# Fused adaLN block: the feed-forward input turned by VectorE block transposes through DRAM instead of by TensorE

## Chip, cores and metric

The kernel runs on one core of a Trainium2 chip. The metric is the device time of one launch in microseconds. TensorE (PE) does the matrix products, VectorE (DVE) and ScalarE (ACT) the elementwise work, GpSimd (POOL) adds and subtracts, and SyncE (SP) issues nearly all DMAs.

## What is computed

Input x is (1, 8192, 512). Two halves follow each other, each behind a LayerNorm with a scale and a shift that come from a modulation vector:

```python
mod = (silu(c) @ wmod)                # sa, ca, ga, sb, cb, gb, each 512 long
h = layernorm(x) * (1 + ca) + sa
x = x + ga * linear_attention(h)      # 16 heads of 32, causal, float32
h = layernorm(x) * (1 + cb) + sb
hid = silu(h @ wg.T) * (h @ wu.T)     # wg, wu: (1536, 512), integer words / 127
x = x + gb * (hid @ wd.T)             # wd: (512, 1536)
```

Products are made with float32 operands split into a high and a low part.

## The kernel before

**Layout.** The attention half goes over 16 groups of 512 tokens and leaves its output in DRAM as `x_mid`. The feed-forward half goes over FG = 8 groups G of 1024 tokens (FT = 8 tiles of 128 tokens) and over HB = 12 blocks q of 128 hidden features. A product needs the features on the partitions, whereas `x_mid` is loaded with the tokens on the partitions. So the normalized x has to be turned: per group eight banks (four feature chunks c, two halves of 512 tokens), each of four 128x128 transposes.

**One step q** (`step` in `tensor`, L1939) is seven products p1, p7, p2, p5, p4, p6, p3 of four matmuls each (a scheme with seven products in place of eight), written by `product` (L1862, its matmul is L1868). p7 and p4 are those of block q-1. ScalarE copies partial results out of PSUM (`save_p1`, `save_p5`, `save_u2`, L1565 to L1578), applies silu (L1583, L1590), and makes the high part of the hidden values (`h_high`, L1595). VectorE adds (`add_c11` L1704, `add_c12` L1710, `add_c22` L1715) and gates (`times_gate1` L1721, `times_gate2` L1729). GpSimd makes the low parts (`h_low`, L1497). What VectorE does for the next group stands in `aside(q)`, between `times_gate1(q-1)` and `add_c12(q)`.

**The down-projections.** After steps 5 and 11 TensorE runs eight of them (`down`, L1910, matmul L1925), numbered i = 0 to 7 and 8 to 15, each of 12 matmuls into one of four banks `dn`. The last p7 and p4 lie between the first ones. `down(G, i)` waits until VectorE has scaled bank i-4 (`gate_y`, L1736). GpSimd then adds the residual (L1502) and SP stores the tile.

**The turn before.** `load_x` (L1396) brings the tiles of group G+2 into `xg` once TensorE has turned group G+1. VectorE takes the statistics in steps 2 to 5 (`norm_stats`, L1681), GpSimd the power -1/2 (`rstd_of`, L1492), VectorE normalizes in place (`norm_x`, L1697) behind `add_c12(6)` and in steps 7 to 9. TensorE turns (`turn`, L1930, transposes L1936) banks 0, 1 and 2 at the ends of steps 8, 9 and 10, bank 3 at the end of step 11, and banks 4 to 7 between down-projections 9 and 11. ScalarE carries each bank with scale and shift to SBUF (`evacuate`, L1562).

**Behind step 11** ("the tail" below) the next group's operands are made: sums T1 to T4 on VectorE (`sum_of`, L1671), high parts on ScalarE (`high`, L1547), low parts on VectorE (`low`, L1675), each for k = 0 and 1. VectorE's order there is written out by hand (L1808 to L1837): twelve sums and low parts and three of the last step's instructions stand ahead of `gate_y(8)`, more between `gate_y(8)`, `(9)` and `(10)`. Only then do down-projections 12, 13 and 14 find their banks free.

**Where the halves meet.** The x of feed-forward group 0 is loaded during attention groups g = 14 and 15 by one 1 MB DMA each (L404), whose statistics are taken in `norm_stats` of the attention part (L757); it is turned by TensorE (L1097, L1105).

Of the kernel before, what the change touches and what calls it, by code (L numbers as in the profile page):

```python
# [43 lines left out]
Shared = namedtuple("Shared", "xg xf h_hi h_lo ring b_hi b_lo full wd silu_sum saved gate h y x_res gb_row pairs sums dn")  # L44
# [24 lines left out]
def build(nc, x, w_qkv, b_qkv, b_cols, w_out, b_out, c_vec, c_row, w_mod, w_mod_t, ffn_words, out):  # L69
    top = ExitStack()  # L70
    with top:
# [10 lines left out]
        k_dram = nc.dram_tensor("k_dram", (P, D), F32, kind="Internal").ap()  # L82
        gb_dram = nc.dram_tensor("gb_dram", (1, D), F32, kind="Internal").ap()
# [60 lines left out]
        ffn = feed_forward(sem, later, ident, mod_col, half_neg, norm, gb_dram, parts, att, shared, x_mid, out)  # L144
# [40 lines left out]
def attention(nc, s, sem, sbuf, psum, ident, gb_dram, mod_col, half_neg, w_hi, w_lo, xt_hi, xt_lo, ga_row,  # L185
# [5 lines left out]
    z_exp = sbuf(s, "z_exp", [P, 2, GN])  # L191
    z_relu = sbuf(s, "z_relu", [P, 2, GN])
# [40 lines left out]
    v_ready, ksum_ready, prod_ready, prod_turned = sem("v_ready"), sem("ksum_ready"), sem("prod_ready"), sem("prod_turned")  # L233
# [26 lines left out]
    shared = Shared([xg[:, t, :] for t in range(GT)] + [z[:, i, :] for z in (z_exp, z_relu) for i in range(2)],  # L260
# [42 lines left out]
    def sync(sp, first_loads):  # L303
# [90 lines left out]
        def group(g, parity):  # L394
# [4 lines left out]
            else:  # L399
# [4 lines left out]
                sp.dma_start(xg[:, :, :], mid_groups[half, :, :, :]).then_inc(x_in, 16)  # L404
# [348 lines left out]
    def vector(dve, sum_of, low):  # L753
        def norm_stats(g, tiles=range(GT)):
            wait(dve, x_in, 16 * (g + 1))
# [568 lines left out]
def feed_forward(sem, later, ident, mod_col, half_neg, norm, gb_dram, parts, att, shared, x_mid, out):  # L1324

    stats, mean_var, var_eps, rstd = norm[1:5]
    xg, xf, h_hi, h_lo, (blocks, filled), b_hi, b_lo, full, wd, total, saved, gate, h, y, x_res, gb_row, xs, sums, dn = shared
# [8 lines left out]
    xt_ps, xf_ready = sem("fxt_ps"), sem("fxf_ready")  # L1336
    gb_in, gb_chain, gb_done = sem("gb_in"), sem("gb_chain"), sem("gb_done")
# [50 lines left out]
    def sync(sp):  # L1388
# [95 lines left out]
    def gpsimd(pool):  # L1484
# [24 lines left out]
        def body(G):  # L1509
            ahead = not isinstance(G, int) or G + 1 < FG  # L1510
            for q in range(HB):
                if q not in (5, 11):
                    h_low(G, q, 1)
                    h_low(G, q, 0)
                if q == 5:
                    h_low(G, q, 1)
                    h_low(G, q, 0)
                    if ahead:
                        rstd_of(G + 1)
# [18 lines left out]
    def scalar(act):  # L1538
# [10 lines left out]
        def evacuate(G, i, bank):  # L1549
# [511 lines left out]
```

## Time and profile before

| | us |
|---|---|
| median of 3 runs | 1996.96 |
| lowest, highest | 1995.05, 2000.71 |
| the profiled execution, its whole time | 1998.45 |
| its span, first to last instruction | 1996.7 |

The mean granted clock of TensorE in the profiled execution is 0.998 of full speed. Attention ends and the feed-forward half begins near 1000 us. A timeline row gives the start, the duration, the engine, the line, the instruction with its output and inputs, how many were merged, and in brackets the idle time before it with what ended it. The programs' names are those of the tensors' memory: pj and sc are PSUM banks of the products, num, sc and state those of the down-projections.

### The profile page before, as it was taken

What the parts mean: (1) busy time and instruction counts of PE and PEld (TensorE: products, weight loads), DVE (VectorE), ACT (ScalarE), POOL (GpSimd) and SP (SyncE); (2) the same over time, 40 slices, a digit from 0 to 9 for tenths busy, and PEclk for the clock granted to TensorE, in tenths of its full rate; (3) what the DMA queues carried; (4) which work ended last, traced back from release to release, by engine and by line L of the source; (5) the groups of instructions that cost most, each with busy time, mean ns of one, the idle gap of its engine ahead of it and who ended that gap; (6) DMA issues with size and microseconds to landing.
All of it is one profiled execution on the core that took longest, in us unless ns stands there. A gap on an engine that the chain in (4) does not pass through costs nothing. (4 is left out here: it accounts for less than half of the span.)

```text
span 1996.7 us, 43856 instructions
## 1 busy us (share of the span) xinstructions
PE 1960.6 (98%) x16008; PEld 1591.9 (80%) x16008; DVE 1443.1 (72%) x2386; ACT 905.7 (45%) x1542; POOL 877.4 (44%) x718
## 2 busy tenths in 40 slices
PE   7999999999999999999899999999999999999999
PEld 4788888888888888887678888788888888888887
DVE  7977888878788878787865857658576585765744
ACT  5443444344444434443344535445354453544533
POOL 2533544444544444453334443444434444344444
PEclk9999999999999999999999999999999999999999
DMA  7223333444434434432575654656546565465553
GB/s 268 69 91 102 115 123 119 135 130 133 135 100 133 128 125 135 127 110 90 179 263 176 207 187 145 214 170 209 186 144 215 171 210 186 144 214 174 169 168 106
DMA packets 202521, 309.81 MB, mean 155 GB/s; under 512 B 16145, under 2 KB 72977, under 8 KB 202386
## 3 DMA queue, kind: packets, MB, share of 16 engines
q1 hardware_dynamic: 201858, 306.78, 48.1%
q8 instruction: 107, 1.75, 0.4%
q10 hardware_dynamic: 528, 1.05, 0.1%
q14 instruction: 28, 0.23, 0.0%
HBM read 225.19 MB, written 82.58 MB: 154 GB/s over the span
## 5 line engine op out<-in xcount | busy, mean ns | idle before, releaser
L1497 POOL TENSOR_TENSOR h_lo<-y_rows,h_hi 128x512 fp32r<-128x512 f32 x192 | 246.5, 1301 | 367.6 <-ACT h_hi L1595 367.6
L461 POOL TENSOR_TENSOR x_res<-y,x_res 128x512 f32<-128x512 f32 x64 | 86.6, 1353 | 294.0 <-DVE y L872 283.5
L851 DVE TENSOR_TENSOR probs<-sc,causal 128x512 f32<-128x512 f32 x256 | 158.5, 681 | 3.8 <-PE sc L1156 2.6
L612 ACT ACTIVATE z_exp<-pj,qk_neg 128x512 f32<-128x512 f32 x128 | 87.7, 686 | 161.5 <-PE pj L1137 158.0
L1137 PE MATMUL pj<-xt_hi,w_hi 128*128 128x512 f32 x512 | 145.9, 406 | 5.7 <-DVE a_t L861 4.7
L1925 PE MATMUL sc<-wd,h_hi 128*128 128x512 f32 x384 | 150.7, 392 | 0.0
L1925 PE MATMUL sc<-wd,h_lo 128*128 128x512 f32 x384 | 149.6, 389 | 0.0
L450 POOL TENSOR_TENSOR a_lo<-a_t,a_hi 128x512 fp32r<-128x512 f32 x60 | 82.2, 1370 | 144.8 <-ACT a_hi L626 144.8
L1137 PE MATMUL pj<-xt_lo,w_hi 128*128 128x512 f32 x512 | 138.1, 391 | 1.8 <-DVE xt_lo L789 1.8
L1137 PE MATMUL pj<-xt_hi,w_lo 128*128 128x512 f32 x512 | 138.1, 392 | 0.0
L1710 DVE TENSOR_TENSOR r_den<-pj,k_tok 128x512 f32<-128x512 f32 x96 | 66.3, 691 | 97.9 <-ACT k_tok L1578 52.2
L1595 ACT ACTIVATE h_hi<-y_rows 128x512 fp32r<-128x512 f32 x192 | 119.0, 620 | 24.9 <-DVE y_rows L1729 13.4
L1573 ACT ACTIVATE k_tok<-sc 128x512 f32<-128x512 f32 x96 | 56.2, 585 | 158.7 <-PE sc L1868 158.7
L445 POOL TENSOR_TENSOR prod<-k_sum,qt 128x512 f32<-128x512 f32 x64 | 94.1, 1471 | 61.4 <-DVE qt L797 42.5
L597 ACT ACTIVATE xf<-sc,mod_col 128x512 f32<-128x512 f32 x64 | 49.8, 778 | 152.7 <-PE sc L1097 152.7
L1137 PEld LDWEIGHTS pj<-xt_hi,w_hi 128*128 128x128 f32 x512 | 91.8, 189 | 33.1 <-DVE a_t L861 11.0
L1137 PEld LDWEIGHTS pj<-xt_lo,w_hi 128*128 128x128 f32 x512 | 96.2, 188 | 23.3 <-DVE xt_lo L789 2.2
L1568 ACT ACTIVATE kv_diag<-pj 128x512 f32<-128x512 f32 x96 | 57.4, 598 | 123.9 <-PE pj L1868 122.9
L1137 PEld LDWEIGHTS pj<-xt_hi,w_lo 128*128 128x128 f32 x512 | 96.7, 189 | 20.9
L1583 ACT ACTIVATE k_sum<-r_den 128x512 f32<-128x512 f32 x96 | 60.7, 632 | 107.7 <-DVE y_rows L1721 95.0
L1721 DVE TENSOR_TENSOR y_rows<-sc,k_sum 128x512 f32<-128x512 f32 x96 | 66.3, 691 | 55.6 <-PE sc L1868 55.6
L1715 DVE TENSOR_TENSOR bv_row<-sc,kv_diag 128x512 f32<-128x512 f32 x96 | 66.3, 691 | 54.8 <-PE sc L1868 54.8
(248 smaller groups left out, 5390.4 us busy)
## 6 DMA issues: line engine op xcount, KB each, us to landing
w_hi<-parts SPq DMA_DIRECT2D x48, 1024.0 KB, 5.4
w_lo<-parts SPq DMA_DIRECT2D x48, 1024.0 KB, 5.4
x_mid<-x_res SPq DMA_DIRECT2D x96, 256.0 KB, 2.8
x_res<-in_L_attn_x SPq DMA_DIRECT2D x64, 256.0 KB, 2.8
k_dram<-k_block SPq DMA_DIRECT2D x252, 64.0 KB
xg<-in_L_attn_x SPq DMA_DIRECT2D x15, 1024.0 KB, 7.4
x_res<-x_mid SPq DMA_DIRECT2D x60, 256.0 KB, 3.9
full<-x_mid SPq DMA_DIRECT2D x60, 256.0 KB, 3.7
```

Source lines behind the costliest of these rows:

```text
L445: pool.tensor_tensor(out=prod[:, c % 2, :], in0=k_sum[:, c % 2, :], in1=qt[parity][:, c, :], op=ALU.mult).then_inc(prod_ready, 1)
L450: pool.tensor_tensor(out=a_lo[:, :], in0=a_t[:, :], in1=a_hi[:, :].bitcast(F32), op=ALU.subtract).then_inc(a_lo_ready, 1)
L461: pool.tensor_tensor(out=x_res[:, slot, :], in0=y[:, :], in1=x_res[:, slot, :], op=ALU.add).then_inc(y_ready, 1)
L612: act.activation(z_exp[:, n % 2, :], pj[:, n % 2, :], ACT.Relu, bias=qk_neg[:, 1 - kind, c:c + 1], scale=-scale).then_inc(below_ready, 1)
L851: dve.tensor_tensor(out=probs[:, h, :].rearrange("p (c i) -> p c i", c=C), in0=sc[:, h, :].rearrange("p (c i) -> p c i", c=C), in1=causal[ ...
L1137: mm = pe.matmul(to, w[:, k, at:at + P], xt[:, k, :], start=(i == 0), stop=(i == len(passes) - 1))
L1497: pool.tensor_tensor(out=h_lo[b], in0=h[i], in1=h_hi[b].bitcast(F32), op=ALU.subtract).then_inc(h_lo_ready, 1)
L1595: act.activation(h_hi[q % 6 * 2 + i], h[i], ACT.Copy).then_inc(h_hi_ready, 1)
L1710: dve.tensor_tensor(out=c12, in0=sums[1], in1=s12, op=ALU.add).then_inc(c12_ready, 1)
L1715: dve.tensor_tensor(out=c22, in0=xs[q % 2], in1=s5, op=ALU.add).then_inc(c22_ready, 1)
L1721: dve.tensor_tensor(out=h[0], in0=xs[q % 2], in1=gate[0], op=ALU.mult).then_inc(h1_ready, 1)
L1925: mm = pe.matmul(dn[i % 4], as_(part[j * 2 + t // GT][:, rows]), as_(wd[half * 6 + j]), start=(j == 0 and part is h_hi), stop=(j == 5 and ...
```

## The change

1. `xg` is now addressed as two contiguous halves of four tiles (`xg_halves`), and a DRAM tensor `xn_dram` is added.
2. SP stores each normalized half into `xn_dram` (`save_xn`, one 1 MB DMA) in its steps 5 and 6 and reads it back (`load_blocks`, four DMAs of 256 KB, runs of 512 bytes) in steps 6 and 7, so that each partition block of 32 holds 32 tokens of a 128-feature stretch.
3. VectorE turns a half with one instruction of 128x2048 elements in 32x32 blocks, in the asides of steps 9 and 10. TensorE's `turn` and its waits are gone.
4. The features are then grouped otherwise on the partitions. The weights and two rows of the modulation matrix are permuted on the host, and the two loads for feed-forward group 0 become 16 DMAs each, in runs of 128 bytes.
5. `evacuate` reads SBUF in place of PSUM. Banks 0, 1 and 2 are evacuated in steps 10, 11 and 11 instead of 9, 10 and 11.
6. The statistics go one step earlier, the variance and `rstd_of` too. `norm_x` goes ahead of `gate_y(0)` (two pairs) and behind `gate_y(3)` and `gate_y(4)`.
7. `add_c22(G, 11)` goes ahead of `sum_of(G + 1, T2, 0)`.
8. `load_x` waits for the evacuations instead of TensorE's transposes.

```diff
...
-                sp.dma_start(xg[:, :, :], mid_groups[half, :, :, :]).then_inc(x_in, 16)
+                for t in range(GT):
+                    for c in range(C):
+                        sp.dma_start(xg[:, t, c * P:(c + 1) * P].rearrange("p (h e) -> p h e", h=HPC),
+                                     mid_groups[half, :, t, :].rearrange("p (h c e) -> c p h e", h=HPC, c=C)[c]
+                                     ).then_inc(x_in, 16)
...
-                wait(sp, xt_ps, (G - 1) * 8)
+                wait(sp, xf_ready, (G - 1) * 8)
...
+        def save_xn(G, second):
+
+            wait(sp, xn_ready, G * 4 + (2 * second - 2))
+            sp.dma_start(xn_dram[second * GN:(second + 1) * GN, :].rearrange("(t p) d -> p t d", p=P),
+                         xg_halves[second][:, :, :]).then_inc(xn_out[second], 16)
+
+        def load_blocks(G, second):
+
+            wait(sp, xn_out[second], G * 16)
+            for h in range(HPC):
+                sp.dma_start(xg_halves[second][h * E:(h + 1) * E, :, :].rearrange("p t (b x) -> p (t b) x", x=P),
+                             xn_dram[second * GN:(second + 1) * GN, h * P:(h + 1) * P].rearrange("(b i) x -> i b x", i=E)
+                             ).then_inc(xb_in[second], 16)
...
+                    if not last and q in (5, 6):
+                        save_xn(G + 1, q - 5)
+                    if not last and q in (6, 7):
+                        load_blocks(G + 1, q - 6)
...
+                if ahead and q == (5 if isinstance(G, int) and G == 0 else 4):
+                    rstd_of(G + 1)
...
-            wait(act, xt_ps, G * 8 + (i - 7))
+            c, second = (k, k + 2, k, k + 2)[which], which // 2
+            wait(act, xt_ps, G * 2 + (second - 1))
...
-            act.activation(to, bank, ACT.Identity, bias=mod_col[:, SB, c:c + 1],
+            turned = xg_halves[second][:, :, :].rearrange("p t (b c i) -> p c (t b) i", c=C, i=E)[:, c, :, :]
+            act.activation(to.rearrange("p (b i) -> p b i", i=E), turned, ACT.Identity, bias=mod_col[:, SB, c:c + 1],
...
-                step(G, q, (lambda i=q - 9: evacuate(G + 1, i, dn[i])) if ahead and q >= 9 else nothing)
+                step(G, q, (lambda: [evacuate(G + 1, i) for i in ((0,), (1, 2))[q - 10]]) if ahead and q >= 10 else nothing)
...
+        def turn(G, second):
+
+            wait(dve, xb_in[second], G * (16 * HPC))
+            blocks = xg_halves[second][:, :, :].rearrange("p t d -> p (t d)")
+            dve.transpose(blocks, blocks).then_inc(xt_ps, 1)
...
-                if ahead and 7 <= q < 10:
-                    norm_x(G + 1, q - 6)
+                if ahead and 9 <= q < 11:
+                    turn(G + 1, q - 9)
...
+            if ahead:
+                norm_x(G + 1, 0)
+                norm_x(G + 1, 1)
             for i in range(FT - 1):
                 gate_y(G, i)
+                if ahead and i in (3, 4):
+                    norm_x(G + 1, i - 1)
...
             sum_of(G + 1, T1, 0)
+            add_c22(G, 11)
             sum_of(G + 1, T2, 0)
-            add_c22(G, 11)
...
-            mm.then_inc(xt_ps, 1)
-
...
-                    if ahead and q >= 8:
-                        wait(pe, y_gated, G * 16 + FT)
-                        turn(G + 1, q - 8, dn[q - 8])
...
+REGROUPED = np.arange(D).reshape(HPC, C, E).transpose(1, 0, 2).reshape(D)
```

## Rows read from the trace of the kernel before

**Rows 1.** the page: busy us (share of the span) xinstructions

```profile
PE 1960.6 (98%) x16008; PEld 1591.9 (80%) x16008; DVE 1443.1 (72%) x2386; ACT 905.7 (45%) x1542; POOL 877.4 (44%) x718
```

**Rows 2.** waits of the weight loads after 1050 us: total, times, longest

```profile
PEld sc L1868 <- ACT k_tok L1578: 11.5, 39, 0.7
```

**Rows 3.** timeline of TensorE at turned banks: start us, us, instruction

```profile
1201.90 0.71 PE L1868 MATMUL sc<-w_hi,w_lo 128*128 128x512 f32 x2
...
1208.39 0.60 PE L1936 MATMUL sc<-ident,xg 128*128 128x128 f32 x4
...
1208.74 0.71 PE L1868 MATMUL sc<-w_hi,w_lo 128*128 128x512 f32 x2
...
1209.29 0.63 PE L1868 MATMUL sc<-xt_hi,w_lo 128*128 128x512 f32 x2
```

**Rows 4.** timeline of TensorE, p7 of two steps that turn nothing

```profile
1267.01 0.72 PE L1868 MATMUL sc<-w_lo 128*128 128x512 f32 x2
...
1273.55 0.72 PE L1868 MATMUL sc<-w_lo,w_hi 128*128 128x512 f32 x2
```

**Rows 5.** timeline of VectorE after step 11, [idle <- releaser]

```profile
1224.18 1.47 DVE L1671 TENSOR_TENSOR full<-xf 128x512 f32<-128x512 f32 x1 [0.44 <-ACT xf L1562]
...
1236.01 0.69 DVE L1736 TENSOR_TENSOR a_t<-num,ga_row 128x512 f32<-128x512 f32 x1
...
1241.84 0.68 DVE L1736 TENSOR_TENSOR a_t<-sc,ga_row 128x512 f32<-128x512 f32 x1
```

**Rows 6.** VectorE in that chain: stretch, length, busy (count), clock, DMA

```profile
1225.69:1242.44 16.75, 16.75 (x22) 1.00 0.32 100
```

**Rows 7.** timeline of TensorE, first matmuls of down-projections 12, 13 and 14

```profile
1237.17 0.39 PE L1925 MATMUL num<-wd,h_hi 128*128 128x512 f32 x1
...
1239.89 0.39 PE L1925 MATMUL sc<-wd,h_hi 128*128 128x512 f32 x1
...
1242.61 0.46 PE L1925 MATMUL sc<-wd,h_hi 128*128 128x512 f32 x1
```

**Rows 8.** one line: the 32x32 block transposes of attention, min/median/max ns

```profile
L845 DVE STREAM_TRANSPOSE k_block<-kt x63: 662/670/714, 63.4 to 972.8; 128x512 f32<-128x512 f32 x63
```

**Rows 9.** timeline of VectorE in step 9, before and after its aside

```profile
1206.86 0.69 DVE L1721 TENSOR_TENSOR y_rows<-sc,k_sum 128x512 f32<-128x512 f32 x1 [0.61 <-PE sc L1868]
...
1209.37 0.69 DVE L1710 TENSOR_TENSOR r_den<-pj,k_tok 128x512 f32<-128x512 f32 x1 [0.91 <-PE pj L1868]
```

**Rows 10.** timeline of ScalarE in step 11: the second turned bank evacuated

```profile
1223.38 0.77 ACT L1562 ACTIVATE xf<-sc,mod_col 128x512 f32<-128x512 f32 x1
```

**Rows 11.** timeline of the DMA issues in the last two attention groups

```profile
895.78 0.39 SPq L404 DMA_DIRECT2D xg<-x_mid  x1
...
907.55 1.78 SPq L319 DMA_DIRECT2D k_dram<-k_block  x4
...
956.47 0.39 SPq L404 DMA_DIRECT2D xg<-x_mid  x1
```

**Rows 12.** the page, DMA issues: count, KB each, median us to landing

```profile
x_mid<-x_res SPq DMA_DIRECT2D x96, 256.0 KB, 2.8
```

**Rows 13.** timeline of VectorE: the first statistics on those two loads

```profile
908.02 1.86 DVE L757 BATCH_NORM_STATS2 stats<-xg 128x6 f32<-128x512 f32 x3
...
962.17 1.29 DVE L757 BATCH_NORM_STATS2 stats<-xg 128x6 f32<-128x512 f32 x2 [0.45 <-DMA xg<-x_mid]
...
965.28 0.42 DVE L861 TENSOR_TENSOR a_t<-num,r_den 128x256 f32<-128x256 f32 x1 [0.96 <-PE pj L1181]
```

**Rows 14.** DMA from 906 to 909.4 us: queue, packets, MB, share of 16 engines

```profile
q1 hardware_dynamic: 288, 0.13, 14.6%
```

**Rows 15.** timeline of TensorE in the last attention group

```profile
977.55 1.74 PE L1206 MATMUL pj<-w_hi,a_hi 128*128 128x512 f32 x4 [2.76 <-DVE a_lo L782]
```

**Rows 16.** two stretches: length, busy PE, PEld, DVE, ACT, POOL, clock, DMA

```profile
966.00:970.00 4.00, 2.02 (x30) 1.60 (x23) 3.83 (x10) 1.11 (x2) 2.15 (x3) 1.00 0.93 311
...
979.00:981.00 2.00, 2.00 (x6) 1.52 (x5) 2.00 (x4) 0.00 (x0) 0.00 (x0) 0.50 0.93 257
```

More of the change, by code:

```diff
@@ L143, in build @@
                                       x_mid, k_dram, parts, downs)
-        ffn = feed_forward(sem, later, ident, mod_col, half_neg, norm, gb_dram, parts, att, shared, x_mid, out)
+        ffn = feed_forward(sem, later, mod_col, half_neg, norm, gb_dram, parts, att, shared, x_mid, xn_dram, out)
         block = top.enter_context(nc.Block())
@@ L259, in attention @@
     flat_diag = kv_diag[:, :, :].rearrange("p c f -> p (c f)")
[L260 removed]
+    shared = Shared([xg[:, t, :] for t in range(GT)] + [z[:, i, :] for z in (z_exp, z_relu) for i in range(2)], [xg, z],
                     [xf[:, 0, :], xf[:, 1, :], r_den[0][:, 0, :], r_den[0][:, 1, :]],
@@ L754, in norm_stats @@
         def norm_stats(g, tiles=range(GT)):
-            wait(dve, x_in, 16 * (g + 1))
+            wait(dve, x_in, 16 * (g + 1) if not isinstance(g, int) or g < NG else 16 * (NG + GT * C * (g - NG + 1)))
             for t in tiles:
@@ L1321, in attention, with feed_forward @@
     return Programs(sync, gpsimd, scalar, vector, tensor), signals, shared
-def feed_forward(sem, later, ident, mod_col, half_neg, norm, gb_dram, parts, att, shared, x_mid, out):
+def feed_forward(sem, later, mod_col, half_neg, norm, gb_dram, parts, att, shared, x_mid, xn_dram, out):
     stats, mean_var, var_eps, rstd = norm[1:5]
-    xg, xf, h_hi, h_lo, (blocks, filled), b_hi, b_lo, full, wd, total, saved, gate, h, y, x_res, gb_row, xs, sums, dn = shared
+    xg, xg_halves, xf, h_hi, h_lo, (blocks, filled), b_hi, b_lo, full, wd, total, saved, gate, h, y, x_res, gb_row, xs, sums, dn = shared
     c11, c12, c22 = total
@@ L1336, in feed_forward @@
     xt_ps, xf_ready = sem("fxt_ps"), sem("fxf_ready")
+    xn_out, xb_in = [sem(f"xn_out{i}") for i in range(2)], [sem(f"xb_in{i}") for i in range(2)]
     gb_in, gb_chain, gb_done = sem("gb_in"), sem("gb_chain"), sem("gb_done")
@@ L1636, in body @@
             high(G + 1, T4, 0)
-            for i, bank in ((4, sums[0]), (5, sums[1]), (6, xs[0]), (7, xs[1])):
-                evacuate(G + 1, i, bank)
+            for i in range(4, 8):
+                evacuate(G + 1, i)
             for op in (B11, B21, T1, T2, B22, T3, T4):
@@ L1774, in aside @@
                     norm_stats(G + 1, 2 * q - 7)
-                if ahead and not first and 2 <= q < 6:
-                    norm_stats(G + 1, q - 2)
-                if ahead and q == 5:
+                if ahead and not first and 1 <= q < 5:
+                    norm_stats(G + 1, q - 1)
+                if ahead and q == (5 if first else 4):
                     norm_var(G + 1)
-                if ahead and 7 <= q < 10:
-                    norm_x(G + 1, q - 6)
+                if ahead and 9 <= q < 11:
+                    turn(G + 1, q - 9)
             if not isinstance(G, int) or G > 0:
@@ L1793, in body @@
             add_c12(G, 6)
-            if ahead:
-                norm_x(G + 1, 0)
             for q in range(7, HB):
@@ L1928, in down @@
                 mm.then_inc(dn_ps, 1)
-        def turn(G, i, bank):
-            k, which = divmod(i, 4)
-            c, second = (k, k + 2, k, k + 2)[which], which // 2
-            wait(pe, xn_ready, G * 4 + (2 * second - 2))
-            for t in range(GT):
-                mm = pe.transpose(bank[:, t * P:(t + 1) * P], xg[second * GT + t][:, c * P:(c + 1) * P], ident[:, :])
-            mm.then_inc(xt_ps, 1)
         def step(G, q):
@@ L2049 @@
         if name == "L0_wmod":
-            layouts.append(("in_wmod_t", a.T))
+            turned = np.ascontiguousarray(a.T).reshape(6, D, D)
+            for m in (SB_MOD, CB_MOD):
+                turned[m] = turned[m, REGROUPED]
+            layouts.append(("in_wmod_t", turned.reshape(6 * D, D)))
         for label, a in layouts:
```

33 lines of the change are left out of this document (8 added, 25 removed).

## The prediction

> **What bounds the kernel now.** I read the profile's page first: TensorE is busy for 98% of the span and VectorE for 72% [rows 1]. A share this high says only that TensorE is the place to save; whether a matmul that is taken out shortens anything depends on which wait ends last behind it. So the waits come next. In the feed-forward half TensorE's matmuls are hardly ever late, but 39 times a weight load waited for ScalarE's copy `save_u2`, 11.5 us in all [rows 2]: where nothing is turned, the chain p4, `times_gate1`, silu, `h_high`, `save_u2`, p7 is a trace longer than the three products beside it. Last comes the tail behind step 11. There VectorE has no idle time from 1225.69 to 1242.44 us [rows 6], and down-projection 14 starts at 1242.61, just behind `gate_y(10)`, which ends at 1241.84 + 0.68 = 1242.52 [rows 5, 7]. In the steps TensorE is the bound; in the tail TensorE and VectorE arrive together, to 0.1 us.
>
> **The turns in the steps.** From the start of a turned bank to the second pair of matmuls behind it is 1209.29 - 1208.39 = 0.90 us [rows 3]. Two matmuls take 0.455 of it, since twelve of a down-projection take 2.72 [rows 7], 0.227 each. A bank thus costs 0.445 us. But a step with a turn lasts 1208.74 - 1201.90 = 6.84 us [rows 3] and one without 1273.55 - 1267.01 = 6.54 [rows 4]: only 0.30 goes, because the wait for `save_u2`, which the turn had covered, comes back. Banks 0, 1 and 2 stand between steps: 3 x 0.30 = 0.9 us for each of the seven groups that turn ahead, 6.3 us. The upper bound is 3 x 0.445 x 7 = 9.3.
>
> **The turns in the tail.** Banks 3 to 7 stand behind step 11 and ahead of down-projection 12: 5 x 0.445 = 2.2 us that TensorE no longer spends. I give all of it back. Down-projections 12, 13 and 14 wait for `gate_y(8)`, `(9)` and `(10)`, and these stand at the end of VectorE's list, whose instructions all stay. Today `gate_y(8)` ends at 1236.01 + 0.69 = 1236.70 and down-projection 12 starts at 1237.17 [rows 5, 7], so 0.4 us of slack is there, none at 14. TensorE will come 2.2 us earlier and wait about 1.8 us at 12, 0.2 at 13 and 0.2 at 14; number 14 starts at the same distance from step 11 as now. Does the list start later? The sum T1 waits for the second evacuation [rows 5], which now runs behind the first one in step 11 and not alone. Its slot starts at 1223.38 and lasts 0.77 [rows 10], so the second ends some 0.65 later. But T1 took 1.47 us where an add with PSUM input takes 0.69 [rows 5, 9], because GpSimd held their shared access to SBUF (a reading of mine: only instructions with two SBUF inputs show it, while GpSimd runs); the 0.65 falls into that wait. `add_c22(11)` now stands ahead of T2, which needs the late evacuation 3, so p4(11) finds its input. Term: 0, bounds -15.4 us (2.2 x 7, if VectorE's list were shorter than I read it) and +7.7 (a further collision of 1.1 us in each group; of the two instructions that I count as caught by GpSimd the longer loses that much).
>
> **VectorE's new work.** One block transpose of 128x512 takes 0.67 us, and at most 0.71 with GpSimd at work beside it [rows 8]; four times the columns give 2.3 to 2.7 us. In step 9 the aside has 1209.37 - 1207.5 = 1.9 us [rows 9], so `add_c12` comes 0.4 to 0.8 us later. Behind it on VectorE queue `add_c22` and `add_c11`. p5 of the next step needs `add_c12`, and it is three products of 0.91 us away, against 0.69 for the add itself: hidden. What follows (silu, `save_p1`, `add_c11`, p6) has about as much. Term 0, bounds 0 to 14 x 0.3 = +4. The `norm_x` pairs move into the first down-projections, where VectorE only waits for TensorE's banks; the steps get no longer without them. The power goes before `h_low(4)` on GpSimd, whose input comes a step later.
>
> **DMA and SP in the loop.** Each group adds two stores of 1 MB and eight loads of 256 KB. A 256 KB issue lands in 2.8 us [rows 12]; four times that is 11 us, and from the first store to its transpose lie three steps of 6.5 us. What SP has queued behind these waits are weight loads for blocks four steps ahead and stores of tiles. `load_x` waits for evacuation 7, but SP reaches it only after storing tile 10, whose `gate_y` comes late anyway [rows 5]. Term 0.
>
> **The two loads where the halves meet.** They are 16 DMAs each now. Four DMAs of k together hold SP for 1.78 us [rows 11], 0.445 each, so 16 hold it for 7.1 us. The last of the first load is issued at 895.78 + 15 x 0.445 = 902.5 and lands 2.8 us later at the latest [rows 12], at 905.3; its statistics start at 908.02 [rows 13]: hidden. The second starts at 956.47, its last part is issued at 963.1 and lands at 965.9, but VectorE takes the statistics at 962.17, already on this load's heels [rows 11, 13]. It is 3.8 us late. Behind the statistics on VectorE wait `gate_y` and the division that TensorE's next out-projection needs; of the 3.8 us, 0.96 of idle time before that division swallows a part [rows 13], so 2.9 us remain. TensorE then stands idle for about 4.9 us (it is idle for 1.98 of the 4 us from 966 now [rows 16]). After an idle stretch of 2.76 us its clock was at 0.50, that is 1.2 instead of 2.4 GHz [rows 15, 16]; from 977.55 to about 981 this costs 1.7 us, and I add it once. Term 2.9 + 1.7 = +4.6 us. Bounds: 0, if the parts land as early as the single DMA did. Above, the nearest packets are those of k, 512 bytes each: 0.146 x 16 x 3.4 us / 288 = 27.6 ns [rows 14]. If 128 bytes took as long, 8192 pieces over 16 engines would take 14.1 us, starting about 1.5 us after the issue: 972.1 for the second load, 9.9 late, 8.9 after the same idle time, and 911.4 for the first, 3.4 late. With the clock +14.0. I take the issue-bound value, since a quarter of the bytes should cost at most half of 27.6 ns, and at 14 ns the transfer takes 7.1 us like the issuing.
> The Trainium skill speaks against these loads (DMA: Bandwidth & Descriptors, Specifications): transfers below 512 bytes fall under line rate, being read, modified and written. No run so far has 128-byte runs. By that rule the upper value would hold and the sum would be +7.7 us in place of -1.7.
>
> **The sum.** -6.3 + 0 + 0 + 0 + 4.6 = -1.7 us. The profiled execution took 1998.45 us, 1.5 above the median of 1996.96; its 1996.75 after the change stands for a median of 1995.3. What a measurement of this kernel can tell from no change is about 0.3%, 6 us: faster means below 1991.0, slower above 2003.0.
>
> **The rivals.**
> A, the forecast: steps gain 6, the tail gives all back, the meeting of the halves costs 4.6: 1995.3, alone 1991 to 2000. Chance 0.42.
> B, the tail gives its part too, as the list there is not what holds down-projection 12. Against it: 16.75 busy of 16.75 us [rows 6]. For it: the order of GpSimd's and VectorE's collisions may come out shorter. -6.3 - 15.4 + 4.6: 1979.9. Chance 0.08.
> C, the loads cost nothing, as they land early enough: -6.3, 1990.7. Chance 0.14. Against it stands the 0.45 us that VectorE waits already [rows 13].
> D, the other side: the 128-byte pieces are bound by the DMA engines, not by SP. Place: both loads; price up to 14.0 us in place of 4.6; it decides from about 14 ns a piece on, and the kernel is slower by over 6 us from some 25 ns on. -6.3 + 14.0 = +7.7: 2004.7. Chance 0.16, for which only the row of 27.6 ns speaks. The rule of the Trainium skill above is this case.
> E, slower too: the 1.8 us wait in each tail brings TensorE to half clock. A stretch with 1.98 us idle in 4 kept 1.00, one idle of 2.76 us did not [rows 15, 16], and the new wait lies beside the first. 7 x 1.7 = 11.9 on top of A: 2007.2. Chance 0.12.
> F, the block transposes run over their slot and hold p5 or p6, and one more collision in the tail: +4 to +10 over A, about 2002. Chance 0.08.
>
> **Numbers.** The range goes from 1987 (C with the upper bound of the steps and part of B) to 2008 (E); outside it stays B and what is beyond D and E. Faster by over 0.3%: B 0.08, C and the lower edge of A 0.13, together 0.21. Slower: D 0.13, E 0.11, F 0.03, together 0.27. Within: 0.52.
>
> **What would show it.** Steps 8 to 10 at 6.54 us (right), or 6.84 (a new wait took the turn's place). A TensorE idle of 1.8 us ahead of down-projection 12, released by `gate_y(8)`, and VectorE again without idle time there (tail); no such idle would be B. The granted clock in those stretches decides E. The statistics of the second load waiting until about 966, and SP busy for 7 us with the 16 issues (A), or landing beyond 970 (D), or at 962 (C). A block transpose of over 2.8 us, or `add_c12` as releaser of a waiting p5, is F. I am wrong altogether if a wait appears in the first half of a group, where I count nothing.

## The result, and the profile after

The changed kernel takes 2026.42 us (median of 4 runs, 2023.98 to 2030.89), the kernel before 1996.72 (1995.05 to 2000.71): ratio 1.0149, 95% interval 1.013 to 1.0167. It is 30 us slower. The forecast was 1995.3 in a range of 1987 to 2008; the time lies above it. The profiled execution took 2028.48 us with a span of 2026.8, against 1998.45 and 1996.7 before.

First the page's busy times, then the waits of TensorE's matmuls that bear on the change (total us, times, longest), and VectorE's block transposes with the idle time ahead of them.

```profile
PE 1954.0 (96%) x15784; PEld 1571.6 (78%) x15784; DVE 1478.6 (73%) x2400; ACT 905.8 (45%) x1542; POOL 885.9 (44%) x718
```
```profile
PE pj L1902 <- DVE r_den L1741: 15.8, 13, 3.9
PE num L1959 <- DVE a_t L1767: 13.8, 7, 2.1
PE pj L1211 <- DVE a_lo L787: 9.6, 3, 7.4
```
```profile
L1729 DVE STREAM_TRANSPOSE z<-z 128x2048 f32<-128x2048 f32 x7 | 16.2, 2312 | 19.9 <-DMA z<-xn_dram 19.9
L1729 DVE STREAM_TRANSPOSE xg<-xg 128x2048 f32<-128x2048 f32 x7 | 16.2, 2311 | 9.3 <-DMA xg<-xn_dram 9.3
```

TensorE is busy 6.6 us less than in [rows 1] and yet its share fell from 98 to 96%: the 224 transposes are gone, and more than their time has come back as waiting. Two of the three waits are new: p5 of steps 10 and 11 waits for `add_c12` (L1741), 13 times, and down-projection 12 waits for `gate_y(8)` (L1767), 7 times. The third has grown: an out-projection near the meeting of the halves waits 7.4 us (L787), where it waited 1.98.

The third fence names what stands behind the first wait. Each of the 14 block transposes takes 2.31 us, as forecast, but VectorE had waited for the read-back 29.2 us in all before it could begin them. One group in full, VectorE first, then TensorE.

```profile
1221.74 2.31 DVE L1729 STREAM_TRANSPOSE xg<-xg 128x2048 f32<-128x2048 f32 x1 [1.65 <-DMA xg<-xn_dram]
1223.98 0.65 DVE L1741 TENSOR_TENSOR r_den<-pj,k_tok 128x512 f32<-128x512 f32 x1
...
1230.18 2.31 DVE L1729 STREAM_TRANSPOSE z<-z 128x2048 f32<-128x2048 f32 x1 [2.38 <-DMA z<-xn_dram]
1232.41 0.65 DVE L1741 TENSOR_TENSOR r_den<-pj,k_tok 128x512 f32<-128x512 f32 x1
```
```profile
1224.68 0.73 PE L1902 MATMUL pj<-w_hi,w_lo 128*128 128x512 f32 x2 [0.70 <-DVE r_den L1741]
...
1233.12 0.73 PE L1902 MATMUL pj<-w_hi 128*128 128x512 f32 x2 [1.43 <-DVE r_den L1741]
...
1252.02 0.50 PE L1959 MATMUL num<-wd,h_hi 128*128 128x512 f32 x1 [2.07 <-DVE a_t L1767]
```

From one transpose to the next are 1230.18 - 1221.74 = 8.44 us, a step being 6.54 [rows 4]. VectorE waits 2.38 us for the data, and behind the transpose `add_c12` stands, which p5 of the next step waits for. `add_c12` can slip as much as the products ahead of p5 last; the 2.3 us of the transpose fit into that, the wait on top of it doesn't. The DMA queue shows why the data are late: SP's issues in that group, and then the issues of the loop by count, KB each and median us to landing.

```profile
1206.85 0.59 SPq L1416 DMA_DIRECT2D xn_dram<-z  x1
1207.55 6.25 SPq L1423 DMA_DIRECT2D xg<-xn_dram  x4
1213.92 1.95 SPq L1399 DMA_DIRECT2D w_hi<-parts  x1
1216.22 5.77 SPq L1423 DMA_DIRECT2D z<-xn_dram  x4
```
```profile
xn_dram<-z SPq DMA_DIRECT2D x7, 1024.0 KB, 8.9
xg<-xn_dram SPq DMA_DIRECT2D x28, 256.0 KB, 10.0
z<-xn_dram SPq DMA_DIRECT2D x28, 256.0 KB, 10.2
```

A load of 256 KB in runs of 512 bytes to 32 partitions lands after 10.0 us, where one of 256 KB in rows of 2 KB lands after 2.8 [rows 12]; and four of them hold SP for 5.8 to 6.3 us. Two things make up the 10 us, and the DMA view of two stretches of this group tells them apart: first 1210 to 1213.5 us, then 1215.6 to 1219.

```profile
DMA packets 446, 1.17 MB, mean 334 GB/s; under 512 B 16, under 2 KB 16, under 8 KB 445
```
```profile
DMA packets 1298, 0.65 MB, mean 190 GB/s; under 512 B 36, under 2 KB 1298, under 8 KB 1298
```

The loads of `xg` begin to be issued at 1207.55, but until 1213.5 the engines move packets of 2.6 KB on average. I take them for those of the store issued just ahead, so that the read-back stands behind it; e3 below bears this out. Then come its own packets, of 512 bytes, and they run at 190 GB/s where the store had 334. By 1215.6 a part has been moved, and the last lands at 1221.7. The loads of the second half, issued from 1216.22 on, stand behind that and behind a weight load.

The meeting of the halves in the changed kernel, SP, VectorE and TensorE:

```profile
895.35 11.71 SPq L407 DMA_DIRECT2D xg<-x_mid  x16
...
959.02 11.12 SPq L407 DMA_DIRECT2D xg<-x_mid  x16
```
```profile
972.64 1.29 DVE L762 BATCH_NORM_STATS2 stats<-xg 128x6 f32<-128x512 f32 x2 [8.37 <-DMA xg<-x_mid]
```
```profile
911.74 1.87 PE L1161 MATMUL sc<-qt,kt 32*128 32x128 f32 x32 [3.06 <-issue]
...
976.62 2.08 PE L1211 MATMUL pj<-w_hi,a_hi 128*128 128x512 f32 x4 [7.45 <-DVE a_lo L787]
```

The same two matmuls in the kernel before:

```profile
910.69 1.17 PE L1156 MATMUL sc<-qt,kt 32*128 32x128 f32 x32 [1.58 <-issue]
...
968.60 1.20 PE L1206 MATMUL pj<-w_hi,a_hi 128*128 128x512 f32 x4 [1.98 <-DVE a_lo L782]
```

The 16 issues take 0.73 us each in the first load and 0.70 in the second, and not 0.445. At the first load TensorE waits 3.06 us where it waited 1.58, and its granted clock is at 0.50 behind that (32 matmuls take 1.87 us in place of 1.17). So the second load is issued 2.55 us later (959.02 against 956.47). Its statistics start at 972.64 (962.17 in [rows 13]), and TensorE stands 7.45 us behind them where it stood 1.98.

Where the 30 us went I read from TensorE's timeline. I compare when the first matmul of certain down-projections starts in both kernels (for instance 1035.57 before and 1042.75 after for the first of the feed-forward half, so 7.2 us). That cuts the run into three kinds of stretch: up to that first one ("entry"); from the last down-projection group of a group's first half to the first of its tail, which holds steps 7 to 11 with banks 0 to 3 ("steps", 7 groups that turn ahead); and from there to the next group's first ("tail", with banks 4 to 7). In us, after minus before:

```
                     entry   steps, 7 groups   tails, 7 groups   down-projections of first halves
forecast             +4.6    7 x -1.35 = -9.4  7 x +0.45 = +3.1  0
after                +7.2    +15.7             +5.7              0.0
  of these by group          6.3 1.8 1.3 1.4 1.2 2.1 1.6   -0.7 1.3 1.7 0.5 0.5 1.7 0.6
```

The forecast line is the one of the prediction in these terms: banks 0 to 3 leave the steps (3 x 0.30 + 0.445), and what bank 3 saves is given back in the tail. 28.6 us stand here; the last 1.5 lie in the last group, behind its first down-projection. So of the miss 25 us are in the steps, 2.6 in the tails and 2.6 at the entry. The first group loses 6.3 us in its steps because its wait for `add_c12` is 3.95 us long and the granted clock is at 0.50 from 1103.2 to 1110.0 us. The entry scatters by itself: between kernels with the same code there it differs by up to 2 us, so smaller differences in that column say nothing.

### The profile page after: what moved, and what is told of

Read it like the earlier page. It is cut to its first block and busy times, and to the rows that moved or that the text cites. A ratio compares the mean times of both kernels' runs of the same rounds, so it can differ in the third digit from the quotient of the medians.

```text
span 2026.8 us, 43425 instructions
## 1 busy us (share of the span) xinstructions
PE 1954.0 (96%) x15784; PEld 1571.6 (78%) x15784; DVE 1478.6 (73%) x2400; ACT 905.8 (45%) x1542; POOL 885.9 (44%) x718
## 5 line engine op out<-in xcount | busy, mean ns | idle before, releaser
L1521 POOL TENSOR_TENSOR h_lo<-y_rows,h_hi 128x512 fp32r<-128x512 f32 x192 | 252.5, 1334 | 377.6 <-ACT h_hi L1620 377.5
L617 ACT ACTIVATE z<-pj,qk_neg 128x512 f32<-128x512 f32 x128 | 87.8, 686 | 162.8 <-PE pj L1142 152.7
L1741 DVE TENSOR_TENSOR r_den<-pj,k_tok 128x512 f32<-128x512 f32 x96 | 65.7, 685 | 95.2 <-ACT k_tok L1603 55.8
```

The source lines that it names most:

```text
L617: act.activation(z_exp[:, n % 2, :], pj[:, n % 2, :], ACT.Relu, bias=qk_neg[:, 1 - kind, c:c + 1], scale=-scale).then_inc(below_ready, 1)
L1521: pool.tensor_tensor(out=h_lo[b], in0=h[i], in1=h_hi[b].bitcast(F32), op=ALU.subtract).then_inc(h_lo_ready, 1)
```

## The experiments

**Is it the read-back?** Three kernels take away what makes it late, each in another way. e1 reads back in one transfer of 2 KB rows (which leaves the regrouping out):

```
-            for h in range(HPC):
-                sp.dma_start(xg_halves[second][h * E:(h + 1) * E, ...] <- xn_dram[..., h * P:(h + 1) * P] ...
+            sp.dma_start(xg_halves[second][:, :, :], xn_dram[second * GN:(second + 1) * GN, :] ...)
```

> The changed kernel, but each half is read back with one DMA of 1 MB in 2 KB rows over all 128 partitions, in the same places (this leaves out the regrouping, so the feed-forward x is another one; the amount of work is the same). Theory R (the read-back in 512-byte runs to 32 partitions at a time lands about 10 us after its issue, too late for the transposes in steps 9 and 10): VectorE no longer waits ahead of the transposes, steps 8 to 10 come down to about 6.6 us, and the time falls from 2026 to about 2001. Theory V (the 2.3 us transposes themselves crowd VectorE's step): the time stays within 3 us of 2026. Theory B (it is the bytes that are too many, not their shape): it falls by less than 8 us.

e5 has no trip through DRAM at all; VectorE turns its own tiles:

```
-                    if not last and q in (5, 6):
-                        save_xn(G + 1, q - 5)
-                    if not last and q in (6, 7):
-                        load_blocks(G + 1, q - 6)
```

> The changed kernel without the trip through DRAM: no stores to and no reads from it, VectorE transposes the blocks of the normalized halves in place as soon as they are normalized (this leaves out the exchange between partition blocks). Theory R: as in the run with wide rows, about 2001, since nothing is left that can be late. Theory V: still 2023 to 2029, with p5 waiting for add_c12. Theory B: 2001 here, but not in the run with wide rows.

e3 computes the whole, with the same transfers, only earlier: the second half is stored behind tile 5, the first half read back behind the last tile of the first half, the second in step 6.

```
-                    if not last and q in (5, 6):
-                        save_xn(G + 1, q - 5)
-                    if not last and q in (6, 7):
-                        load_blocks(G + 1, q - 6)
+                    if not last and q == 5:
+                        save_xn(G + 1, 0)
+                    if not last and q == 6:
+                        load_blocks(G + 1, 1)
...
+                    if not last and i == 5:
+                        save_xn(G + 1, 1)
+                    if not last and i == FT - 1:
+                        load_blocks(G + 1, 0)
```

> The changed kernel with the second store issued behind tile 5 of the first half's stores, the first read-back behind tile 7 and the second read-back in step 6: each 3 to 9 us earlier, same bytes, same runs. Theory R: the waits of VectorE for the blocks vanish, 2003 to 2008. Theory B (bandwidth): the reads now collide with the x_res loads, GpSimd waits for these and the time stays above 2018.

Measured: e1 2003.45 us (ratio 1.0028, interval 1.0018 to 1.0038), e5 2002.87 (1.0034, 1.0021 to 1.0046), e3 2005.93 (1.0047, 1.0031 to 1.0064). e1 and e5 lie 2 us above the 2001 of their theory, far from the rivals. In all three the waits for `add_c12` are gone. The transposes of e3, and all of TensorE's waits of e3 in its second tail:

```profile
L1733 DVE STREAM_TRANSPOSE z<-z 128x2048 f32<-128x2048 f32 x7 | 16.1, 2302 | 0.0
L1733 DVE STREAM_TRANSPOSE xg<-xg 128x2048 f32<-128x2048 f32 x7 | 16.1, 2301 | 0.0
```
```profile
1243.53 0.50 PE L1963 MATMUL num<-wd,h_hi 128*128 128x512 f32 x1 [2.07 <-DVE a_t L1771]
```

The stretches, in us against before (falls: tails in whose records the granted clock goes below full):

```
        entry   steps   tails   falls of 7
after   +7.2    +15.7   +5.7    3
e1      +7.6     -9.1   +6.4    3
e5      +7.8     -9.1   +4.0    2
e3      +8.5     -8.7   +5.7    3
```

All three agree, so it is the lateness of the read-back that cost 24 us in the steps, with the fall of the clock in the first group that came of it: not the 2.3 us of the transposes, which all three keep, and not the traffic, which e3 keeps. With the data there in time a group gains 1.24 to 1.30 us, the forecast having 1.35. e3 also shows how the transfer's price depends on what stands ahead of it. The same eight issues in SP's queue, and the landing times of all of them:

```profile
1201.26 1.95 SPq L1423 DMA_DIRECT2D xg<-xn_dram  x4
1203.33 1.43 SPq L1399 DMA_DIRECT2D w_lo<-parts  x1
1204.80 5.83 SPq L1423 DMA_DIRECT2D z<-xn_dram  x4
```
```profile
xg<-xn_dram SPq DMA_DIRECT2D x28, 256.0 KB, 5.8
```

Four issues take 1.95 us when the engines have little to do, and 5.83 right behind the first four and a weight load. The start times of the two traces can't be compared as they stand, since e3 is 6 us ahead by then. Counted from the start of the group's down-projection 7, the first four start only 0.4 us sooner than in the changed kernel (10.15 against 10.59 us) and the last four 5.6 us sooner (13.7 against 19.3). Yet the first four land after 5.8 us and not 10.0: the 1 MB store that stood right ahead of them is 7 us earlier in the queue. So the store ahead made up over 4 of the 10 us. The last four, behind the first four and a weight load, still take about 10 us.

**The entry loads alone.** Both loads as one transfer of 1 MB each, as before (this leaves the regrouping of the first group out); the loop is that of the changed kernel.

```
-                for t in range(GT):
-                    for c in range(C):
-                        sp.dma_start(xg[:, t, c * P:(c + 1) * P] ... <- mid_groups[half, :, t, :] ... [c])
+                sp.dma_start(xg[:, :, :], mid_groups[half, :, :, :]).then_inc(x_in, 16)
```

> The changed kernel, but the two loads for feed-forward group 0 are one DMA of 1 MB each again (group 0 gets its features in the old order, which leaves out its regrouping). Theory: the start of the feed-forward half lies 7.2 us later in the changed kernel's trace, and all of it comes from these loads: 2019. Rival: the 7.2 us are mostly the longer low-clock stretch, which stays: 2023 or more.

Measured: 2017.66 us (1.0102, 1.0086 to 1.0119), 8.8 under the changed kernel. The entry is at -0.9 in place of +7.2, the steps at +13.3. So the loads cost about 8 us, nearly twice the term of the forecast.

**What is there to be won at all?** In the kernel before, TensorE's turns are left out and nothing stands in their place (ScalarE's evacuations read the tiles in SBUF).

```
-            for t in range(GT):
-                mm = pe.transpose(bank[:, t * P:(t + 1) * P], xg[second * GT + t][:, c * P:(c + 1) * P], ident[:, :])
-            mm.then_inc(xt_ps, 1)
+            pe.sem_inc(xt_ps, 1)
```

> The kernel before, with TensorE's 32 transposes of each of the 7 later groups left out, and nothing put in their place: ScalarE copies the unturned tiles, so the output isn't the reference's. It says what the change has to win at most in that half. Theory: 0.30 us for each of 8 banks, 2.4 us a group, less what the tail gives back because TensorE then comes to down-projection 12 before its bank is read: steps 9 to 11 win 1.3 a group, as in e3 and e5, the tail nothing, sum 7 x 1.3 = 9 us: 1986 to 1990 us. Rival (the four tail banks are won too): 7 x 2.4 = 17 us: 1980 us. Rival (the tail gives back more than it won, with falls of the clock as in e1 to e5): 1990 to 1996 us.

Measured: 1989.31 us (0.9957, 0.9941 to 0.9972), steps -9.1, tails -1.6. The waits of the tail, over the 7 groups:

```profile
PE num L1925 <- DVE a_t L1736: 8.7, 7, 1.3
PE sc L1868 <- DVE bv_row L1715: 1.9, 7, 0.3
```

Banks 4 to 7 leave each tail stretch, 7 x 4 x 0.445 = 12.5 us in all, and 8.7 + 1.9 = 10.6 come back as waits for VectorE's list; 1.9 stay, against 1.6 measured. What the steps win is nearly all there is. By the medians it is 8.4 us (1997.76 - 1989.31), before any new work has a price.

**Is the tail bound by the order of VectorE's list, or by its length?** e6 is e3 with `gate_y(8)` and `gate_y(9)` ahead of low parts that stood before them:

```
-            for op in (T2, B22, T3, B11, B21, T4):
-                low(G + 1, op, 0)
-            sum_of(G + 1, T1, 1)
-            gate_y(G, FT)
+            low(G + 1, T2, 0)
+            low(G + 1, B22, 0)
+            low(G + 1, T3, 0)
+            gate_y(G, FT + 0)
+            low(G + 1, B11, 0)
+            low(G + 1, B21, 0)
+            gate_y(G, FT + 1)
+            low(G + 1, T4, 0)
+            sum_of(G + 1, T1, 1)
...
```

> e3_early_back (2005.9 us) with one more edit, in VectorE's hand-written list of the tail: the reads of down-projection banks 12 and 13 (gate_y 8 and 9) are moved ahead of 3 and 1 low parts of the next group's operands. In e3 TensorE stands 2.1 us at down-projection 12 of every one of the 7 tails behind that read, and the tail gives back 5.7 us in all. Theory T (the length and order of VectorE's list bounds the tail, since PE's turns left it): the wait at down-projection 12 falls to under 0.5 us, the clock doesn't fall in the tails, and the time is 1990 to 1997 us, 9 to 15 us under e3. Rival T2 (VectorE's work is back to back for 20 us there, so what is moved ahead pushes the operands' low parts out and TensorE waits for them, or for c11, instead): 2004 to 2008 us, with the 2 us wait under another name. Rival T3 (half of each): 1998 to 2003 us.

e8 is e6 with the second of the two entry loads whole; VectorE regroups its features as it normalises, from `xg` to `z`:

```
+                if half:
+                    sp.dma_start(xg[:, :, :], mid_groups[half, :, :, :]).then_inc(x_in, 16)
...
+                if isinstance(g, int) and g == NG + 1:
+                    out = z[:, t, :].rearrange("p (c h e) -> p c h e", c=C, h=HPC)
+                    src = src.rearrange("p (h c e) -> p c h e", h=HPC, c=C)
```

> e6_early_tail with the second of the two entry loads (the one that feeds tiles 4 to 7 of the first feed-forward group) back as one 1 MB transfer; the features are regrouped by VectorE as it normalises, from xg into z, and turn_second reads z. The first load keeps its 16 transfers. Theory L (the 16 issues of 0.70 us hold the statistics back, at 972.6 us instead of 965.3 in after, and TensorE stands behind them at 976 with the clock falling): 4 to 6 us under e6, the start of the feed-forward half 2.5 to 3.5 us later than before instead of 8. Rival (a write in runs of 32 elements costs VectorE more than a plain one and shows up at the same place): 0 to 2 us under e6.

e9 is e8 with all four reads early, after the times at which e6's rows say they are wanted:

```
+            gate_y(G, FT + 1)
+            low(G + 1, T4, 0)
+            sum_of(G + 1, T1, 1)
+            gate_y(G, FT + 2)
+            sum_of(G + 1, T2, 1)
+            sum_of(G + 1, T3, 1)
+            gate_y(G, FT + 3)
+            sum_of(G + 1, T4, 1)
+            low(G + 1, B11, 1)
...
```

> e8_all (2004.5 us) with another order of VectorE's list in the tail, laid out from e6's rows: there the reads of banks 12 and 13 came in time and the 2.4 us wait went to the read of bank 14. In e3 and e6 a down-projection of the tail takes TensorE 2.7 us, so the reads have to end by about 1366.5, 1369.3, 1372.1 and 1374.8 on the clock of e3's second tail; the new order reads bank 12 behind 3 low parts, bank 13 behind 2 more, bank 14 behind 1 low part and 1 sum, bank 15 behind 2 sums, and has the remaining 7 low parts and the last sum behind all four. Theory T (the order of the list bounds the tail): TensorE waits under 0.5 us in every tail, the clock doesn't fall there, the tail gives back under 0.3 us a group, and with 9.1 us won in the steps and 3.6 lost at the entry the time is 1989 to 1994 us, under that of the kernel before. Rival T2 (the low parts that are pushed out are wanted by the next group's first products): a wait of 1 to 3 us a group on a low part takes its place: 1999 to 2006 us.

Measured: e6 2010.76 us (1.0064, 1.005 to 1.0077), e8 2004.53 (1.0034, 1.0023 to 1.0044), e9 2003.32 (1.0033, 1.002 to 1.0045). My theory of the order falls, and e6 lies above the range of its rivals too: its tails give back 11.3 us in place of e3's 5.7, with five falls of the clock in place of three. The one wait of each tail moved with the list: to down-projection 14 in e6, and to the next group's first product, which needs the low part of B11, in e9.

```profile
PE sc L1967 <- DVE a_t L1771: 16.9, 7, 2.5
```
```profile
PE sc L1915 <- DVE xt_hi L1709: 15.3, 7, 2.2
```

So the order isn't what bounds the tail: with `gate_y(8)` late in the list the wait is 2.07 us, with it earlier 2.4, with all four reads early 2.2. That leaves the length of the list, as the prediction said, and when it starts (e12 below); no run here shortened it. e8 against e6 puts the second entry load at 6.2 us, e11 against e10 below at only 3.8.

**The one part of the change that is left: c22 ahead of T2.** e10 is e3 with the order of the kernel before, e14 the changed kernel with it.

```
-            add_c22(G, 11)
             sum_of(G + 1, T2, 0)
+            add_c22(G, 11)
```

> e3_early_back (2005.9 us) with the order of add_c22 and the sum T2 as in the kernel before. Theory: the sum T2 runs 0.7 us earlier and c22 0.7 us later, nobody is bound by either, so all else stays: 2005 to 2007 us, the wait at down-projection 12 still 2.1 us. Rival (c22 ahead of T2 is what keeps banks or products free in time): 2008 us or more, with a TensorE wait on c22.

> The changed kernel with one part undone: the last add_c22 stands behind the sum T2 again, as in the kernel before. In e10 against e3 that alone gave 6 us: TensorE's 2.07 us wait at down-projection 12 became two, 0.83 and 1.26 us, with no fall of the clock behind them, and GpSimd's two low parts of h ran 1 us apart instead of back to back beside VectorE's low parts. Theory: the same here, 4 to 7 us under the changed kernel: 2019 to 2023 us, still with the waits for the read-back in the steps. Rival (with the read-back late, VectorE's list starts late whatever its order): 2024 to 2028 us.

Measured: e10 1999.86 us (1.0013, 1.0004 to 1.0022), 6.1 under e3; e14 2022.96 (1.0136, 1.012 to 1.0151), 3.5 under the changed kernel, though the intervals of the two overlap. For e10 both the theory (no effect) and the rival (slower) fall. Its second tail on TensorE, and the waits over all 7:

```profile
1232.81 0.73 PE L1906 MATMUL sc<-w_hi 128*128 128x512 f32 x2 [0.83 <-DVE bv_row L1750]
...
1242.52 0.50 PE L1963 MATMUL num<-wd,h_hi 128*128 128x512 f32 x1 [1.26 <-DVE a_t L1771]
```
```profile
PE num L1963 <- DVE a_t L1771: 8.7, 7, 1.3
PE sc L1906 <- DVE bv_row L1750: 5.7, 7, 0.8
```

TensorE waits as long as in e3, 0.83 + 1.26 = 2.09 us against 2.07, but in two pieces ten us apart. What differs is the clock. These are two stretches of that tail in e3 (the first holds the wait of 2.07 us, the second lies behind it) and one of the same tail in e10, which holds the wait of 1.26 (length, busy PE, PEld, DVE, ACT, POOL, granted clock, DMA). A granted clock of 0.5 is the lower level, 1.2 GHz in place of 2.4:

```profile
1239.00:1247.00 8.00, 5.93 (x20) 4.38 (x19) 8.00 (x12) 5.53 (x10) 3.68 (x3) 0.81 0.04 15
1244.00:1247.40 3.40, 3.40 (x10) 2.64 (x9) 3.40 (x5) 2.30 (x4) 3.40 (x2) 0.51 0.21 75
```
```profile
1238.00:1246.00 8.00, 6.74 (x30) 5.28 (x29) 8.00 (x13) 5.98 (x10) 3.38 (x2) 1.00 0.13 51
```

In the kernels whose tail has one long wait the clock fell in 27 of 56 tails (after 3, e1 3, e2 2, e3 3, e5 2, e6 5, e8 5, e9 4). The wait is 1.9 to 2.5 us in 55 of them, and 1.4 in the first tail of the changed kernel, where the clock held. In the kernels where the wait is split, or is 1.3 us and at most a short one beside it (e4, e10, e11, e12, e14), it fell in none of 35. The waits of kernels with falls are otherwise alike to about 0.1 us from tail to tail, so what decides between the two outcomes the traces don't show. A tail with a fall gives back 1.3 to 1.9 us where the others of the same kernel give back -0.7 to 0.6, in after, e1, e3 and e5. So the order of c22 leaves the total wait as it is; what changes with it is whether the clock can fall. I can't say by these runs that it explains all of the 6.1 us: three falls of 1.3 are 3.9 of them in the profiled executions, which lie 4.6 apart.

**Together.** e11 is e10 with the whole second entry load of e8; e12 is e11 with turns and first evacuations one step earlier.

> e10_c22_back (1999.9 us) with the second entry load as one 1 MB transfer, as in e8. Theory: the two are additive, the tail stays at 2.8 us given back with no fall of the clock, the entry falls from 7.8 to about 3: 1994 to 1997 us. Rival (the 5 us of e8 against e6 were luck of the clock, since the clock falls at 975 in e10 too): 1998 to 2000 us.

The edit of e12 beyond e11:

```
-                if ahead and 9 <= q < 11:
-                    turn(G + 1, q - 9)
+                if ahead and 8 <= q < 10:
+                    turn(G + 1, q - 8)
...
-            evacuate(G + 1, 3)
```

> e11_c22_entry with the turns one step earlier (steps 8 and 9 in place of 9 and 10) and the first four evacuations too (one behind step 9, two behind step 10, one behind step 11, none ahead of the tail's list on ScalarE). In e10 VectorE waits 1.18 us for the last of these evacuations before its 20 us list of the tail starts, and TensorE then waits 0.83 us for c22 and 1.26 us for bank 12. Theory T (the tail is bounded by when VectorE's list begins and how long it is, whatever its order): the list starts 1.0 to 1.5 us earlier, TensorE's wait at bank 12 falls to about 0.3 us and the tail gives nothing back: 7 x 1.0 = 7 us under e11, 1987 to 1990 us. Rival (the list then meets the two low parts of h on GpSimd earlier and is slowed by them all the same, or evacuations in step 11 hold ScalarE's copies back): within 2 us of e11.

Measured: e11 1996.03 us (0.999, 0.9981 to 0.9999), e12 2016.13 (1.01, 1.0085 to 1.0116).

```
        entry   steps   tails   falls of 7
e10     +7.8     -9.1   +2.8    0
e11     +4.2     -9.1   +2.7    0
e12     +6.1    +11.6   -2.1    0
```

The parts add up in e11. It is the best version with the turns on VectorE, 1.5 us under the kernel before (1997.51 beside it), which can hardly be told from no change. In e12 the tails gave back 4.8 us less than in e11, 0.7 a group where the theory had 1.0. Of the two waits it was c22's that went, and not the one at bank 12, which stayed 1.3 where the theory had 0.3. In the second tail VectorE's list starts 1.2 us sooner than in e11, counted from the first down-projection of the tail, but its second sum then takes 1.67 us in place of 0.69, with GpSimd at work: in part it is the rival. The steps lost 21 us, which neither theory nor rival had: one step earlier the data are late again.

```profile
PE pj L1910 <- DVE r_den L1749: 12.3, 12, 1.9
PE num L1967 <- DVE a_t L1775: 8.8, 7, 1.3
```
```profile
1233.78 1.67 DVE L1704 TENSOR_TENSOR full<-r_den,full 128x512 f32<-128x512 f32 x1
...
1343.97 2.31 DVE L1737 STREAM_TRANSPOSE z<-z 128x2048 f32<-128x2048 f32 x1 [2.15 <-DMA z<-xn_dram]
```

That is the read-back's mechanism a fourth time, from the other side: e11 and e12 have the same issues at the same places, and what changed is when their data are wanted.

The entry in e11, SP, VectorE and TensorE:

```profile
960.41 0.40 SPq L406 DMA_DIRECT2D xg<-x_mid  x1
```
```profile
966.41 1.29 DVE L764 BATCH_NORM_STATS2 stats<-xg 128x6 f32<-128x512 f32 x2 [0.79 <-DMA xg<-x_mid]
```
```profile
911.76 2.09 PE L1166 MATMUL sc<-qt,kt 32*128 32x128 f32 x32 [3.46 <-issue]
...
972.51 1.90 PE L1216 MATMUL pj<-w_hi,a_hi 128*128 128x512 f32 x4 [1.98 <-DVE a_lo L792]
```

The wait of 7.45 us is down to 1.98, what the kernel before has. TensorE's idle stretch of 3.46 us ahead of 911.76 is left (1.58 before), at the first load, which keeps its 16 transfers. In the changed kernel SP is held until 907 there, and k's stores and loads stand behind it in its queue. That this lengthens the stretch is read from the order of the rows; no run takes this load alone away. e2, which takes both away, has 1.59 us there again.

## Why the prediction was wrong

**DMA and SP in the loop (term 0): this step failed.** It priced the read-back of the normalized x, which VectorE's transposes wait for, by the nearest row of the same size, 256 KB in 2.8 us [rows 12], and took four of them as 11 us. That row has rows of 2 KB to 128 partitions. The load has 512-byte runs to 32 partitions, moves at 190 GB/s, stands behind a 1 MB store, and lands after 10 us; four hold SP for 6 us. The store's own time it didn't price at all. Three steps of 6.54 us, 19.6 in all, were to be enough from store to transpose. In the group shown the second half takes 23.3 us from the issue of its store (1206.85) to the landing of its last part, just ahead of the transpose at 1230.18. For all other terms without a row I had given bounds, for this one none. Measured by e1, e5 and e3: +24 to 25 us in place of 0, by way of p5 waiting for `add_c12`. The prediction also asked what p5 can bear of a late `add_c12`, and answered only for the transpose's own length.

**The turns in the steps (-6.3 for banks 0 to 2).** Right: with bank 3, 1.24 to 1.30 us a group measured against 1.35, once the data are in time, and the same in e4 where nothing takes their place.

**The tail (term 0, waits of 1.8, 0.2 and 0.2).** Right in its mechanism and its size: one wait of 2.07 us at down-projection 12 released by `gate_y(8)`, 0 at 13 and 14, so 2.07 against 2.2. e4, e6 and e9 show that it isn't the list's order: 1.5 to 2.5 us a group come back in all of them. The late second evacuation costs nothing, as said: T1 takes 0.73 us in the changed kernel and not 1.47. Rival B (the tail's part is won too) had 8% and is refuted.

**Rival E, the clock.** It was to fall in every tail, 7 x 1.7. It falls in 3 of 7 in the changed kernel and costs about 1.3 each. As a case of its own it was mis-sized; as a part of the forecast it was missing from the sum, +4.

**The entry loads (+4.6).** The mechanism is the one named, SP is held by the 16 issues; the size is 7 to 8. Two terms were off. The first load was counted as hidden, while its issues hold SP for 11.7 us, TensorE waits 3.06 us and not 1.58, and the clock falls: the second load starts 2.55 us later for it. And an issue takes 0.70 us and not 0.445, which is 3.8 us more by the sixteenth. Together they bring the statistics from 965.9 to 972.2, and 972.64 was measured. Rival D (the pieces are bound by the DMA engines at 27.6 ns) named nearly the time, 972.1, by another cause: from 960 to 970 us 7127 packets took 62.0% of 16 engines, 0.62 x 16 x 10 us / 7127 = 13.9 ns each, half of D's. By that the 8192 pieces need 7.1 us, less than the 11.1 us of their issuing, and the engines stand idle for a good third of the time. D's 972.1 was also counted from a load that starts at 956.47; that it came out near the measured time is chance. The line of the DMA view it rests on:

```profile
q1 hardware_dynamic: 7127, 1.08, 62.0%
```

**VectorE's new work (term 0), rival F.** Right: 2.31 us a transpose, forecast 2.3 to 2.7, and in e3 and e5 nothing waits for `add_c12`.

## What to carry to other kernels

Price a transfer by a row of its own shape (bytes per run, partitions, what runs beside it), and where there is none give it bounds and look for what its data hold up; the size in KB says little. Count what stands ahead of it in its queue as part of the price. An operation that is moved off the bounding engine gains only where that engine is the bound alone: where a second one ends level with it, the time comes back as a wait, and here three other orders of the second one's list only moved that wait. Whether a shorter list gives it back no run here tested. If such a wait can't be avoided, two short ones ten us apart did better here than one of 2 us, since the clock held behind the short ones.

## What the runs showed of the hardware

The cost of issuing isn't constant: one and the same issue of 256 KB in 512-byte runs took SP 1.95 / 4 = 0.49 us with the engines nearly idle and 5.83 / 4 = 1.46 behind others, and one of 64 KB in 128-byte runs 0.70, where 64 KB in 512-byte runs took 0.445 [rows 11]. Not every issue behind others is held: e1's read-back, one issue of 1 MB in 2 KB rows right behind the same store, took 0.45.

```profile
1200.92 0.45 SPq L1422 DMA_DIRECT2D xg<-xn_dram  x1
```

Runs of 512 bytes moved at 190 GB/s in the stretch shown above, with the queue full, and the packets of 2.6 KB ahead of them at 334. The Trainium skill (DMA: Bandwidth & Descriptors, Specifications) gives 512 bytes as the least size for line rate; by these rows a run of just that size had little over half of what packets of 2.6 KB had. It isn't the direction, since e1 reads the same data back in 2 KB rows at 377 GB/s (1209.5 to 1211.5 us):

```profile
DMA packets 384, 0.75 MB, mean 377 GB/s; under 512 B 16, under 2 KB 16, under 8 KB 384
```

Whether the size of the run or the 32 partitions of a transfer does it, no run here tells apart, since e1 changed both.

A wait of TensorE of 1.9 to 2.5 us in one piece let the granted clock fall to 0.5 in 27 of 55 tails; about the same length in two pieces, 0.5 to 0.9 and 1.2 to 1.3 us, in none of 21.
